# Cross attention on one core: the transposed probabilities' parts are made ahead of the second piece of the token-major context

## The chip, the core and the metric

The kernel runs on one core of a Trainium2 chip. The metric is the device time of one execution in microseconds, as the median of several runs.

## The reference, cut to what matters

The whole network is a layer norm, a decoder layer (self attention, cross attention over a context, feed-forward) and a two-expert gated feed-forward, for 8 batches of 100 tokens of width 512. The change touches the cross attention:

```
cscores = einsum('btd,bmd->btm', q1, k2) / sqrt(512)         # 8 x 100 x 722
ca      = einsum('btm,bmd->btd', softmax(cscores), v2)       # memory: 8 x 722 x 512
x       = _ln(x + ca, g2, be2)
```

The kernel multiplies the context itself with the probabilities first, and applies the value weights later (its unit U_CV).

## The kernel before

Nearly every fp32 operand is split in two parts, a high one (rounded to the matmul's format, made by ScalarE with a copy) and a low one (the operand minus the high part, made by DVE or POOL with a subtraction), and each product is three matmuls: high x high, high x low, low x high. Names end in H and L for the parts and in R for what was loaded.

The cross attention is a loop over the 8 batches b. Each engine has its program written out by hand, in order, and the engines wait for each other by semaphores only. For a batch the context is used twice: feature-major (ctR, ctH, ctL; two pieces) for the scores, and token-major (cnR, cnH, cnL; three pieces of 256 token rows, i = 0, 1, 2) for the value product. There is one buffer each of cnR, cnH and cnL, and two of ctH and ctL.

- TensorE (block `tensor`): `cross_attend(b)`, the value product, 18 matmuls at L750 to L752, six for each piece of cn; then `cross_prob_transpose(b + 1)` (L737, 6 transposes), `cross_scores(b + 2)` (L724 to L726, 24 matmuls; from b = 6 on half of the unit U_CV instead, 24 matmuls at L576 to L578), and `cross_attend_transpose(b)` (L762, 4 transposes).
- ScalarE: `split_cn` copies cnR to cnH (L919), `cross_attended` scales the value product into utok (L1011), `cross_probT` copies the transposed probabilities to ptH (L1003), `split_ct` makes ctH (L912), `cross_exp` the exponential prob (L995), `cross_attendedT` AH (L1016).
- DVE: `split_cn` makes cnL of pieces 0 and 1 (L1179), `cross_recip` srec (L1341), `cross_probT` the low part ptL of the transposed probabilities (L1335), `cross_max` the maximum in three small instructions, the last of which writes snb (L1327, L1328, L1330), `split_ct` ctL (L1174), `cross_attendedT` AL (L1345).
- POOL makes cnL of piece 2 (L493), one per batch from batch 1 on.
- SP issues the loads: a piece of cnR or ctR is asked for when its low part has been made from the piece before.

The value product of batch b waits for ptL of batch b at its start, and for each piece's cnL as it comes to it:

```python
def cross_attend(b):
    pe.wait_ge(c_probT_low, b + 1)
    ...
    for c in range(MC):
        wait_cn_low(pe, b, c // 2)
```

`wait_cn_low` waits for POOL's count for piece 2 and for DVE's count for pieces 0 and 1. ScalarE's copy into cnH waits for the piece's transfer and for the chunks of the value product before that read the same piece. utok waits for all six chunks of its batch. The exponential of a batch waits for snb.

Of the kernel before, what the change touches and what calls it, by code (L numbers as in the profile page):

```python
# [113 lines left out]
def build(nc, x, ctxt, ctxn, wvo, wts, consts, g3, be3, out):  # L114
    with ExitStack() as ctx:
# [203 lines left out]
        def raw(ap):  # L319
            return ap.bitcast(F32)  # L320
# [565 lines left out]
        def _(act):  # L886
            def split_weights(n, k):
                raw_weights = WRK if n == U_K else WR
                if n == U_Q and k == 0:
                    act.wait_ge(w0_loaded, 16)  # L890
                elif n == U_Q and k == 2:
                    act.wait_ge(weights_loaded, 16)
                elif n == U_K:
                    act.wait_ge(wk_loaded, 16)
                elif k == 0:
                    act.wait_ge(weights_loaded, 16 * LOADED.index(n))
                if k == 0 and BEFORE[n] is not None:
                    m, h = ORDER[LAST[BEFORE[n]]]
                    act.wait_ge(gemm_done, gemm_count(m, h, KC - 1))
                elif k == 0 and SLOT[n] == 2:  # L900
                    act.wait_ge(ct_low, 2 * B)
                    for i in (1, 2):
                        wait_cn_low(act, B - 1, i)
                act.activation(WH[SLOT[n]][:, k, :], raw_weights[:, k, :], ACT.Copy).then_inc(w_high, 1)  # L904

            def split_ct(b, i):
                act.wait_ge(ct_loaded[i], 16 * (b + 1))
                if b == 1:
                    act.wait_ge(to_feat, 16)
                if b >= 2:  # L910
                    act.wait_ge(c_scores, b - 1)
                act.activation(ctH[b % 2][:, 2 * i:2 * i + 2, 0:M], ctR[:, 2 * i:2 * i + 2, :],  # L912
                               ACT.Copy).then_inc(ct_high, 1)

            def split_cn(b, i):
                act.wait_ge(cn_loaded[i], (16 if i < 2 else 48) * (b + 1))
                if b >= 1:
                    act.wait_ge(c_chunk, MC * (b - 1) + 2 * i + 2)
                act.activation(cnH[:, 2 * i:2 * i + 2, :], cnR[:, 2 * i:2 * i + 2, :],  # L919
                               ACT.Copy).then_inc(cn_high, 1)  # L920

            def unit(n, h, groups=range(KC)):
                for e in groups:
                    src = ps[:, bank(n, h, e), 0:HALF]
                    kind = KINDS[n]
                    if act_writes(n):
                        act.wait_ge(gemm_done, gemm_count(n, h, e))
                    if kind == "fp32":
                        dst, col = (qT, C_BQ) if n == U_Q else (kT, C_BK)
                        act.activation(half(dst, h, e), src, ACT.Identity,  # L930
                                       bias=cst[:, col + e:col + e + 1]).then_inc(act_evac, 1)
                    elif kind == "split":
                        act.activation(half(AH, h, e), src, ACT.Identity, bias=gv[:, e:e + 1]).then_inc(act_evac, 1)
                    elif kind == "relu_bias":
                        col = C_B1 + KC * ((n - U_F) // 2) + e
                        act.activation(half(AT, h, e), src, ACT.Relu, bias=cst[:, col:col + 1])  # L936
                        act.activation(half(AH, h, e), src, ACT.Relu,  # L937
                                       bias=cst[:, col:col + 1]).then_inc(act_evac, 1)
                    elif kind == "relu":
                        act.activation(half(AH, h, e), src, ACT.Relu).then_inc(act_evac, 1)  # L940
                    if POS[n, h] in SPLIT_AT:
                        for k in [[0, 1], [2], [3], []][e]:
                            split_weights(SPLIT_AT[POS[n, h]], k)
# [47 lines left out]
            def cross_exp(b):  # L991
                act.wait_ge(c_max, b + 1)
                if b >= 2:
                    act.wait_ge(c_probT, b - 1)
                act.activation(prob[b % 2][:, 0:M].rearrange("p (i m) -> p i m", i=2), ps[0:T, 4:6, 0:MH],  # L995
                               ACT.Exp, bias=snb[:, b:b + 1], scale=SCALE,
                               accum_out=ssum[:, b:b + 1]).then_inc(c_exp, 1)

            def cross_probT(b):
                act.wait_ge(c_probT, b + 1)  # L1000
                if b >= 2:
                    act.wait_ge(c_chunk, MC * (b - 1))
                act.activation(ptH[b % 2][:, :].rearrange("p (i m) -> p i m", i=2), ps[:, 6:8, 0:3 * T],  # L1003
                               ACT.Copy).then_inc(c_probT_high, 1)

            def cross_attended(b):
                act.wait_ge(c_chunk, MC * (b + 1))
                act.wait_ge(c_rec, b + 1)
                if b >= 2:
                    act.wait_ge(c_attT, b - 1)  # L1010
                act.activation(utok[:, b % 2, :], ps[0:T, 2, :], ACT.Copy,  # L1011
                               scale=srec[:, b:b + 1]).then_inc(c_att_sb, 1)

            def cross_attendedT(b):
                act.wait_ge(c_attT, b + 1)
                act.activation(tokens(AH, b), ps[:, 3, 0:KC * T].rearrange("p (k t) -> p k t", k=KC),  # L1016
                               ACT.Copy).then_inc(c_attT_high, 1)
# [66 lines left out]
            for b in range(B):  # L1084
                if b + 1 < B:
                    split_cn(b + 1, 0)
                    split_cn(b + 1, 1)
                cross_attended(b)
                if b + 1 < B:
                    cross_probT(b + 1)  # L1090
                    split_cn(b + 1, 2)
                if b + 3 < B:
                    split_ct(b + 3, 0)
                if b + 2 >= B:
                    unit(U_CV, 0, [[0, 1], [2, 3]][b + 2 - B])
                if b + 2 < B:
                    cross_exp(b + 2)
                if b + 3 < B:
                    split_ct(b + 3, 1)
                cross_attendedT(b)  # L1100
                if b == B - 2:
                    for k in range(KC):
                        split_weights(U_F, k)
# [53 lines left out]
        def _(dve):  # L1157
# [14 lines left out]
            def split_ct(b, i):  # L1172
                dve.wait_ge(ct_high, 2 * b + i + 1)
                dve.tensor_tensor(ctL[b % 2][:, 2 * i:2 * i + 2, 0:M], ctR[:, 2 * i:2 * i + 2, :],  # L1174
                                  raw(ctH[b % 2][:, 2 * i:2 * i + 2, 0:M]), ALU.subtract).then_inc(ct_low, 1)

            def split_cn(b, i):
                dve.wait_ge(cn_high, 3 * b + i + 1)
                dve.tensor_tensor(cnL[:, 2 * i:2 * i + 2, :], cnR[:, 2 * i:2 * i + 2, :],  # L1179
                                  raw(cnH[:, 2 * i:2 * i + 2, :]), ALU.subtract).then_inc(cn_low, 1)  # L1180
# [152 lines left out]
            def cross_probT(b):  # L1333
                dve.wait_ge(c_probT_high, b + 1)
                dve.tensor_tensor(ptL[b % 2][:, :].rearrange("p (i m) -> p i m", i=2), ps[:, 6:8, 0:3 * T],  # L1335
                                  raw(ptH[b % 2][:, :].rearrange("p (i m) -> p i m", i=2)),
                                  ALU.subtract).then_inc(c_probT_low, 1)

            def cross_recip(b):
                dve.wait_ge(c_exp, b + 1)  # L1340
                dve.reciprocal(srec[:, b:b + 1], ssum[:, b:b + 1]).then_inc(c_rec, 1)  # L1341
# [179 lines left out]
            for b in range(B):  # L1521
                if b + 1 < B:
                    split_cn(b + 1, 0)
                    split_cn(b + 1, 1)
                    cross_recip(b + 1)
                    cross_probT(b + 1)
                if b + 2 < B:
                    cross_max(b + 2)
                if b + 3 < B:
                    split_ct(b + 3, 0)  # L1530
                if b + 2 >= B:
                    unit(U_CV, 0, [[0, 1], [2, 3]][b + 2 - B])
                if b + 3 < B:
                    split_ct(b + 3, 1)
                cross_attendedT(b)
# [87 lines left out]
```

## Time and profile before

| | us |
|---|---|
| median of 3 runs | 532.81 (532.42 to 533.29) |
| profiled execution, its own time | 532.86 |
| span of its trace (first to last instruction) | 531.1 |
| TensorE matmul busy | 519.0 (98% of the span) |
| VectorE (DVE) busy | 325.7 (61%) |
| ScalarE (ACT) busy | 222.0 (42%) |
| GpSimd (POOL) busy | 104.1 (20%) |

The loop of the cross attention lies between about 140 and 214 us of the span. The granted TensorE clock is full (1.00) there. Times in the rows below are microseconds from the start of the span. A row of the timeline gives the start, the duration, the engine, the line, the operation, output<-inputs, and in brackets how long the engine had been idle before it and what released it; where several instructions alike follow each other they are one row with their count. A busy TensorE in these rows is not TensorE at its peak: its matmuls overlap in the records, and starts are what to go by.

### The profile page before, as it was taken

What the parts mean: (1) busy time and instruction counts of PE and PEld (TensorE: products, weight loads), DVE (VectorE), ACT (ScalarE), POOL (GpSimd) and SP (SyncE); (2) the same over time, 40 slices, a digit from 0 to 9 for tenths busy, and PEclk for the clock granted to TensorE, in tenths of its full rate; (3) what the DMA queues carried; (4) which work ended last, traced back from release to release, by engine and by line L of the source; (5) the groups of instructions that cost most, each with busy time, mean ns of one, the idle gap of its engine ahead of it and who ended that gap; (6) DMA issues with size and microseconds to landing.
All of it is one profiled execution on the core that took longest, in us unless ns stands there. A gap on an engine that the chain in (4) does not pass through costs nothing.

```text
span 531.1 us, 7541 instructions
## 1 busy us (share of the span) xinstructions
PE 519.0 (98%) x3014; PEld 496.3 (93%) x3014; DVE 325.7 (61%) x556; ACT 222.0 (42%) x388; POOL 104.1 (20%) x93
## 2 busy tenths in 40 slices
PE   8899999999999999999999999999999999999996
PEld 6799999789988878999999999999999899999996
DVE  3753789895698986877365544277674354442225
ACT  2853542483589865264535153206413231320200
POOL 2430430022032135054006200005530000000000
PEclk9999999999999999999999999999999999999999
DMA  8941212031589961228022222002220033100004
GB/s 231 349 166 57 64 73 79 1 113 56 192 287 325 305 224 34 79 97 227 1 79 80 80 80 79 1 0 81 80 79 1 0 123 117 53 28 0 1 1 123
DMA packets 18428, 53.75 MB, mean 101 GB/s; under 512 B 1625, under 2 KB 2425, under 8 KB 15833
## 3 DMA queue, kind: packets, MB, share of 16 engines
q1 hardware_dynamic: 18332, 53.20, 30.6%
q8 instruction: 24, 0.39, 0.3%
q10 hardware_dynamic: 60, 0.07, 0.1%
q14 instruction: 12, 0.09, 0.1%
HBM read 51.63 MB, written 1.64 MB: 100 GB/s over the span
## 4 chain that ended last, share of the span: by engine, by line
PE 81%; DVE 11%; DMA 3%; ACT 3%; issue 2%; SPq 0%; POOL 0%; DVEq 0%; ACTq 0%
PE ps L576 21%; PE ps L578 21%; PE ps L577 21%; PE ps L611 3%; DMA tok<-x_in 2%; PE ps L589 2%; DVE cnL L1179 2%; PE ps L750 1%; DMA cnR<-ctxn_in 1%; PE ps L752 1%; PE ps L751 1%; PE ps L622 1%; PE ps L724 1%; PE ps L726 1%; PE ps L725 1%
## 5 line engine op out<-in xcount | busy, mean ns | idle before, releaser
L576 PE MATMUL ps<-XH,WH 128*128 128x400 f32 x352 | 122.5, 348 | 0.9 <-DVE AL L1191 0.4
L578 PE MATMUL ps<-XH,WL 128*128 128x400 f32 x352 | 121.5, 345 | 0.0
L577 PE MATMUL ps<-XL,WH 128*128 128x400 f32 x352 | 121.4, 345 | 0.0
L576 PE MATMUL ps<-AH,WH 128*128 128x400 f32 x288 | 100.2, 348 | 0.6 <-DVE AL L1195 0.2
L578 PE MATMUL ps<-AH,WL 128*128 128x400 f32 x288 | 99.4, 345 | 0.0
L577 PE MATMUL ps<-AL,WH 128*128 128x400 f32 x288 | 99.3, 345 | 0.0
L576 PEld LDWEIGHTS ps<-XH,WH 128*128 128x128 f32 x352 | 66.1, 188 | 2.7 <-DVE AL L1191 0.8
L577 PEld LDWEIGHTS ps<-XL,WH 128*128 128x128 f32 x352 | 66.2, 188 | 0.1
L578 PEld LDWEIGHTS ps<-XH,WL 128*128 128x128 f32 x352 | 66.2, 188 | 0.0
L488 POOL TENSOR_TENSOR WL<-WR,WH 128x512 fp32r<-128x512 f32 x38 | 52.4, 1409 | 67.2 <-ACT WH L904 67.2
L576 PEld LDWEIGHTS ps<-AH,WH 128*128 128x128 f32 x288 | 54.1, 188 | 2.1 <-DVE AL L1195 1.9
L577 PEld LDWEIGHTS ps<-AL,WH 128*128 128x128 f32 x288 | 54.1, 188 | 0.0
L578 PEld LDWEIGHTS ps<-AH,WL 128*128 128x128 f32 x288 | 54.1, 188 | 0.0
L1213 DVE TENSOR_TENSOR acc<-ps,acc 128x400 f32<-128x400 f32 x48 | 27.3, 571 | 40.4 <-PE ps L578 40.1
L904 ACT ACTIVATE WH<-WR 128x512 fp32r<-128x512 f32 x80 | 45.9, 627 | 13.5 <-DMA WR<-wts_in 13.5
L936 ACT ACTIVATE AT<-ps,cst 128x400 f32<-128x400 f32 x32 | 19.1, 596 | 76.3 <-PE ps L578 76.2
L940 ACT ACTIVATE AH<-ps 128x400 fp32r<-128x400 f32 x32 | 16.1, 504 | 81.0 <-PE ps L578 81.0
L1198 DVE SCALAR_TENSOR_TENSOR AL<-ps,AH 128x400 fp32r<-128x400 f32 x32 | 18.4, 575 | 42.3 <-ACT AH L940 42.3
L1195 DVE TENSOR_TENSOR AL<-AT,AH 128x400 fp32r<-128x400 f32 x32 | 21.4, 670 | 36.3 <-ACT AH L937 36.1
L1174 DVE TENSOR_TENSOR ctL<-ctR,ctH 128x1444 fp32r<-128x1444 f32 x16 | 26.6, 1660 | 14.2 <-ACT ctH L912 14.2
L1169 DVE TENSOR_TENSOR WL<-WR,WH 128x512 fp32r<-128x512 f32 x40 | 29.9, 767 | 6.4 <-ACT WH L904 6.4
L493 POOL TENSOR_TENSOR cnL<-cnR,cnH 128x1024 fp32r<-128x1024 f32 x7 | 16.8, 2401 | 65.9 <-ACT cnH L919 65.9
(181 smaller groups left out, 817.8 us busy)
## 6 DMA issues: line engine op xcount, KB each, us to landing
WR<-wts_in SPq DMA_DIRECT2D x19, 1024.0 KB, 4.8
ctR<-ctxt_in SPq DMA_DIRECT2D x16, 722.0 KB, 5.0
cnR<-ctxn_in SPq DMA_DIRECT2D x16, 512.0 KB, 5.2
cnR<-ctxn_in SPq DMA_DIRECT2D x8, 256.0 KB
tok<-x_in SPq DMA_DIRECT2D x4, 384.0 KB, 10.4
tok<-x_in SPq DMA_DIRECT2D x1, 1536.0 KB
cnR<-ctxn_in SPq DMA_DIRECT2D x8, 160.0 KB
VR<-wvo_in SPq DMA_DIRECT2D x4, 256.0 KB, 6.2
```

What stands on the lines that cost most here:

```text
L488: pool.tensor_tensor(WL[SLOT[n]][:, k, :], WR[:, k, :], raw(WH[SLOT[n]][:, k, :]), ALU.subtract).then_inc(w_low_pool, 1)
L493: pool.tensor_tensor(cnL[:, 2 * i:2 * i + 2, :], cnR[:, 2 * i:2 * i + 2, :], raw(cnH[:, 2 * i:2 * i + 2, :]), ALU.subtract).then_inc(cn_lo ...
L576: pe.matmul(dst, wh, half(mh, h, k), start=(k == 0), stop=False)
L577: pe.matmul(dst, wh, half(ml, h, k), start=False, stop=False)
L578: mm = pe.matmul(dst, wl, half(mh, h, k), start=False, stop=(k == KC - 1))
L904: act.activation(WH[SLOT[n]][:, k, :], raw_weights[:, k, :], ACT.Copy).then_inc(w_high, 1)
L936: act.activation(half(AT, h, e), src, ACT.Relu, bias=cst[:, col:col + 1])
L1169: dve.tensor_tensor(WL[SLOT[n]][:, k, :], raw_weights[:, k, :], raw(WH[SLOT[n]][:, k, :]), ALU.subtract).then_inc(w_low, 1)
L1174: dve.tensor_tensor(ctL[b % 2][:, 2 * i:2 * i + 2, 0:M], ctR[:, 2 * i:2 * i + 2, :], raw(ctH[b % 2][:, 2 * i:2 * i + 2, 0:M]), ALU.subtrac ...
L1195: dve.tensor_tensor(half(AL, h, e), half(AT, h, e), raw(half(AH, h, e)), ALU.subtract).then_inc(dve_evac, 1)
L1198: dve.scalar_tensor_tensor(out=half(AL, h, e), in0=src, scalar=0.0, in1=raw(half(AH, h, e)), op0=ALU.max, op1=ALU.subtract).then_inc(dve_e ...
L1213: dve.tensor_tensor(half(acc, h, e), src, half(acc, h, e), ALU.add).then_inc(dve_evac, 1)
```

## The change

It moves one piece of work on two engines. On ScalarE the copy of piece 1 (cnH) of the next batch goes from before utok to behind ptH. On DVE the subtraction of piece 1 (cnL) goes from before srec and ptL to behind them. TensorE's, POOL's and SP's programs are untouched, and so is all arithmetic.

```diff
@@ scalar, the loop
             for b in range(B):
                 if b + 1 < B:
                     split_cn(b + 1, 0)
-                    split_cn(b + 1, 1)
                 cross_attended(b)
                 if b + 1 < B:
                     cross_probT(b + 1)
+                    split_cn(b + 1, 1)
                     split_cn(b + 1, 2)
@@ vector, the loop
             for b in range(B):
                 if b + 1 < B:
                     split_cn(b + 1, 0)
-                    split_cn(b + 1, 1)
                     cross_recip(b + 1)
                     cross_probT(b + 1)
+                    split_cn(b + 1, 1)
                 if b + 2 < B:
                     cross_max(b + 2)
```

On DVE, here one iteration of the loop (b = 1; ctL and ptL carry the number of their buffer, "x2" is two instructions alike):

```order
 L1174 TENSOR_TENSOR ctL_79<-ctR,ctH_77 128x2x722 x2
 L1345 TENSOR_TENSOR AL_65<-ps,AH_63 128x4x100
-L1179 TENSOR_TENSOR cnL<-cnR,cnH 128x1024 x2
+L1179 TENSOR_TENSOR cnL<-cnR,cnH 128x1024
 L1341 RECIPROCAL srec<-ssum 100x1
 L1335 TENSOR_TENSOR ptL_86<-ps,ptH_84 128x600
+L1179 TENSOR_TENSOR cnL<-cnR,cnH 128x1024
 L1327 TENSOR_REDUCE smx<-ps 100x1
 L1328 TENSOR_SCALAR smx<-smx,cshift 100x1
```

The second cnL now stands between ptL and the maximum. On ScalarE, the same iteration before the change, from one exponential (prob) to the next:

```order
L995 ACTIVATE prob_82,ssum<-ps,snb 100x722
L912 ACTIVATE ctH_77<-ctR 128x2x722
L1016 ACTIVATE AH_63<-ps 128x4x100
L919 ACTIVATE cnH<-cnR 128x1024 x2
L1011 ACTIVATE utok<-ps,srec 100x512
L1003 ACTIVATE ptH_84<-ps 128x600
L919 ACTIVATE cnH<-cnR 128x1024
L912 ACTIVATE ctH_76<-ctR 128x2x722
L995 ACTIVATE prob_83,ssum<-ps,snb 100x722
```

and with the change:

```order
L995 ACTIVATE prob_82,ssum<-ps,snb 100x722
L912 ACTIVATE ctH_77<-ctR 128x2x722
L1016 ACTIVATE AH_63<-ps 128x4x100
L919 ACTIVATE cnH<-cnR 128x1024
L1011 ACTIVATE utok<-ps,srec 100x512
L1003 ACTIVATE ptH_84<-ps 128x600
L919 ACTIVATE cnH<-cnR 128x1024 x2
L912 ACTIVATE ctH_76<-ctR 128x2x722
L995 ACTIVATE prob_83,ssum<-ps,snb 100x722
```

utok and ptH move forward by one cnH, and the second cnH stands directly ahead of the third.

## Rows read from the trace of the kernel before

**Rows 1.** Windows, each one iteration, from one value product's start to the next's.

```profile
core 0: us, PE busy (x) PEld busy (x) DVE busy (x) ACT busy (x) POOL busy (x), PEclk, DMA share, GB/s
149.40:158.38 8.98, 8.98 (x55) 7.72 (x54) 8.16 (x11) 6.89 (x10) 2.16 (x2) 1.00 0.98 320
...
176.92:186.97 10.05, 9.22 (x52) 7.77 (x52) 9.23 (x11) 8.82 (x12) 3.21 (x2) 1.00 0.90 305
...
196.11:205.52 9.41, 9.41 (x54) 8.17 (x53) 7.52 (x10) 5.33 (x8) 3.95 (x2) 1.00 0.43 148
```

**Rows 2.** Line L750: what ended its engine's idle time (us, times).

```profile
  DVE ptL L1335: 2.2, 3
```

**Rows 3.** Timeline of TensorE: starts of value products and of thirteenth matmuls.

```profile
167.57 0.47 PE L750 MATMUL ps<-cnH,ptH 128*100 128x512 f32 x1
...
170.42 0.39 PE L750 MATMUL ps<-cnH,ptH 128*100 128x512 f32 x1
...
186.97 0.47 PE L750 MATMUL ps<-cnH,ptH 128*100 128x512 f32 x1 [0.84 <-DVE ptL L1335]
...
198.95 0.39 PE L750 MATMUL ps<-cnH,ptH 128*100 128x512 f32 x1
```

**Rows 4.** Timeline of ScalarE: exponentials, and the work between two of them.

```profile
150.85 0.87 ACT L995 ACTIVATE prob<-ps,snb 100x722 f32<-100x722 f32 x1 [1.25 <-DVE snb L1330]
...
160.07 0.87 ACT L995 ACTIVATE prob<-ps,snb 100x722 f32<-100x722 f32 x1
...
160.92 1.40 ACT L912 ACTIVATE ctH<-ctR 128x1444 fp32r<-128x1444 f32 x1
...
162.60 2.00 ACT L919 ACTIVATE cnH<-cnR 128x1024 fp32r<-128x1024 f32 x2
164.50 0.68 ACT L1011 ACTIVATE utok<-ps,srec 100x512 f32<-100x512 f32 x1
...
169.23 0.87 ACT L995 ACTIVATE prob<-ps,snb 100x722 f32<-100x722 f32 x1 [0.22 <-DVE snb L1330]
...
173.79 1.06 ACT L919 ACTIVATE cnH<-cnR 128x1024 fp32r<-128x1024 f32 x1 [0.96 <-DMA cnR<-ctxn_in]
...
198.35 0.86 ACT L995 ACTIVATE prob<-ps,snb 100x722 f32<-100x722 f32 x1 [2.52 <-DVE snb L1330]
```

**Rows 5.** Timeline of POOL in the same iteration: piece 2 of cnL.

```profile
166.77 2.41 POOL L493 TENSOR_TENSOR cnL<-cnR,cnH 128x1024 fp32r<-128x1024 f32 x1 [6.75 <-ACT cnH L919]
```

**Rows 6.** Timeline of DVE in the same iteration.

```profile
164.42 2.35 DVE L1179 TENSOR_TENSOR cnL<-cnR,cnH 128x1024 fp32r<-128x1024 f32 x2
...
166.76 0.76 DVE L1335 TENSOR_TENSOR ptL<-ps,ptH 128x600 fp32r<-128x600 f32 x1
167.44 0.90 DVE L1327 TENSOR_REDUCE smx<-ps 100x1 f32<-100x722 f32 x1
...
168.62 0.58 DVE L1330 SCALAR_TENSOR_TENSOR snb<-cshift,smx 100x1 f32<-100x1 f32 x1
```

**Rows 7.** The chain of work that ended last: transfer of a second piece.

```profile
166.79 6.97 DMA cnR<-ctxn_in
```

**Rows 8.** Timeline elsewhere, and L535 (min/median/max ns): POOL beside DVE with two SBUF inputs.

```profile
283.74 0.69 DVE L1169 TENSOR_TENSOR WL<-WR,WH 128x512 fp32r<-128x512 f32 x1
283.81 1.77 POOL L535 TENSOR_TENSOR tok<-tok,be3b 100x512 f32<-100x512 f32 x1 [37.40 <-PE ps L578]
...
L535 POOL TENSOR_TENSOR tok<-tok,be3b x8: 1274/1684/1768, 283.8 to 294.3; 100x512 f32<-100x512 f32 x8
...
228.28 1.30 POOL L488 TENSOR_TENSOR WL<-WR,WH 128x512 fp32r<-128x512 f32 x1 [7.86 <-ACT WH L904]
228.94 1.07 DVE L1207 TENSOR_TENSOR XS<-XS,XL 128x400 f32<-128x400 f32 x1
229.54 1.62 POOL L488 TENSOR_TENSOR WL<-WR,WH 128x512 fp32r<-128x512 f32 x1
```

## The prediction

> **What bounds the kernel now.** I read the windows of the cross attention loop first. TensorE is busy in practically all of each iteration, so a microsecond is only won where TensorE waits. An iteration in which it waits for nothing takes 8.98 us (149.40 to 158.38, four products of scores, value product, transposes) [rows 1]. The four iterations from 158.38 to 196.11 take 37.73 us, where 4 x 8.98 is 35.92: 1.8 us are lost in them, the most in the one of 10.05 us [rows 1]. The idle time before the value product's matmuls (L750) is put down to one releaser, the low part ptL of the transposed probabilities, 2.2 us over both of TensorE's queues in three places [rows 2], one of them 0.84 us [rows 3]. That is what the change goes for. The next question is what makes ptL late.
>
> Write E(k) for the start of the exponential of batch k on ScalarE. The starts run from 150.85 (k=2) to 198.35 (k=7), with 160.07 and 169.23 between [rows 4]: 47.50 us for five steps, 9.50 each, more than TensorE's 8.98. So another loop is the slower one. One step of it, from 160.07 to 169.23, is 9.16 us, and ScalarE, POOL and DVE pass it on: the exponential, ctH at +0.85, AH, the first two pieces of cnH from +2.53 (162.60), utok and ptH from +4.43 (164.50), the third piece of cnH [rows 4], then POOL's cnL of that piece from 166.77 (+6.70) for 2.41 us, to 169.18 [rows 5], and the exponential of the next batch at 169.23. What ties the last two is DVE's snb: a 100x1 instruction issued at 168.62 that takes 0.58 us and ends at 169.20, right after POOL [rows 6]. It reads two tensors in SBUF while POOL reads SBUF, and does not get through before POOL is done. So E(k+1) = POOL's end + 0.05. ptL ends 7.45 us after E(k) (166.76 + 0.76 against 160.07) [rows 6], and TensorE begins the value product of batch k at 167.57, which is E(k) + 7.50 [rows 3]. Of the 1.70 us by which five steps exceed 5 x 9.16, the rest are steps in which ScalarE waits for the second piece's transfer: it took 6.97 us [rows 7] and kept the copy 0.96 us [rows 4]. At k=2 and k=7 TensorE is behind this loop, between them it goes at the loop's pace.
>
> **The change part by part.** Nothing is added: the same instructions in another order, for b+1 = 1 to 7. On ScalarE the copy of the second piece goes behind utok and ptH. Those three together take as long as before, the third piece's copy ends where it did, and POOL is released at E + 6.70 as before. utok moves forward to about E + 3.5 and waits there for the value product of the batch before, which began at 158.38 [rows 1] and takes 4.2 us (2.85 us for twelve of its eighteen matmuls [rows 3]): done near 162.7, and wanted at 163.5. No new wait. On DVE the second cnL goes behind srec and ptL. The four instructions (cnL, cnL, srec, ptL) run from 164.42 to the start of the maximum at 167.44 in either order. So in the new order ptL is done one cnL earlier, about 1.13 us (half of the pair's 2.27 step), at E + 6.32; and cnL of the second piece ends where ptL ended, about E + 7.46, after beginning at about E + 6.24 [rows 6]. TensorE needs that piece six matmuls into the product, 1.42 us after its start, E + 7.79 at the earliest: 0.3 us to spare. SP's queue asks for the next second piece 0.75 us later than before, but ScalarE wants it 1.14 us later, so the 0.96 us wait of [rows 4] goes. A rest of it up to 0.6 us would cost nothing, because DVE takes the piece at E + 6.24 only.
>
> **The price.** Before, DVE was in ptL (one input in PSUM) when POOL began, and neither minded the other. Now DVE is in a cnL, two inputs in SBUF, from E + 6.24 to E + 7.46 when POOL is released at E + 6.70. No row of before has this pair, but two have its kind. At 283.74 DVE begins a WL of two SBUF inputs and keeps its usual 0.69 us; POOL's sum, released at 283.81, takes 1.77 us where the shortest of its eight is 1.274. DVE's end at 284.43 lies 0.62 into it: 0.50 us longer for an overlap of 0.62 [rows 8]. At 229.54 POOL takes 1.62 instead of 1.30, with DVE's end at 230.01, 0.47 into it: 0.32 us longer [rows 8]. So POOL is held by the overlap less 0.12 to 0.15. Here the overlap is 0.76 us, and the hold 0.62 us. (The Trainium skill, "SBUF — State Buffer", section "Who interferes with whom", says that a DVE instruction with two SBUF inputs contends with a GpSimd instruction that reads SBUF, that whoever issues first has the pair for the whole instruction, and that the other blocks. The rows agree in kind; by the page the hold would be the whole overlap, which is a rival below.)
>
> Through snb the hold enters the slower loop: each step becomes 9.16 + 0.62 = 9.78 us. It is paid six times (the pieces of batches 1 to 6), and the two waits for transfers go. E(7) = 150.85 + 6 x 0.62 + 5 x 9.16 = 200.37, against 198.35. ptL being early doesn't help there: TensorE begins the product of batch k at E(k) + 6.37 at best, and its third piece (the thirteenth matmul, 2.85 us in, as 167.57 to 170.42 shows [rows 3]) is wanted at E(k) + 9.22, while POOL delivers it at E(k) + 9.73. Before, it was wanted at E(k) + 10.35 and there at 9.11. So the wait moves from ptL to POOL's piece, some 0.5 us in each of batches 3 to 6. From the thirteenth matmul of batch 6 (198.95) to the start of batch 7's product (205.52) TensorE works 6.57 us [rows 1, 3]. Now that stretch starts at E(7), as POOL is done then: 200.37 + 6.57 = 206.94, **1.42 us later** than 205.52. Behind that TensorE is continuously busy and sets the pace, so it stays. The profiled execution took 532.86 us (its span is 531.1), and the median of the runs is 532.81, so both can stand as the base: 532.86 + 1.4 = 534.3 us.
>
> **Bounds of the unknown.** The sum moves by six times the hold. With the whole overlap of 0.76 it is +2.3 us, 535.1. With 0.5 it is +0.7. The break-even is 0.62 - 1.42/6 = 0.38 us. With no hold TensorE binds: 158.38 + 4 x 8.98 + 9.41 = 203.70, or -1.8 us. I take 0.62 because two rows of different lengths give the same rule and the pair here differs only in being longer.
>
> **The rivals.**
> (1) *POOL isn't held by this pair, and the gain comes through*: ptL 1.13 us early removes TensorE's waits, 1.8 us, 531.1 us. For it: TensorE's idle time is really put down to ptL [rows 2], and the change does bring ptL forward. Against it: both rows of the kind show POOL longer. It decides where the hold is under 0.38 us. Chance 0.18.
> (2) *A smaller hold, 0.2 to 0.5 us*, because the second cnL begins earlier against POOL than worked out (the hold shrinks as ScalarE is later): the gain at ptL and the loss at POOL cancel, 532.3 to 533.5. Chance 0.20.
> (3) *The full overlap counts*, by the page's rule worked out on these rows as 0.76 us: 535.1 us. Chance 0.12. The same page gives about 115 ns between the end of the DVE instruction and the release; as an estimate by that page the sum would be some 0.7 us more again.
> (4) *The order turns round*: if POOL were released before DVE begins the second cnL (0.46 us of margin), DVE would stand for POOL's 2.41 us, and the maximum with it. One such step costs some 2.4 us: 536.5. snb shows that DVE does stand [rows 6]. Chance 0.03.
> The forecast, a hold of 0.5 to 0.75 us, has the other 0.47.
>
> **How the numbers follow.** About 0.2% (1.07 us) is what a measurement of this kernel tells from no change; the three runs spread over 0.9 us. Faster is rival 1 and a tail of 2: 0.20. Same is the rest of 2 and that part of the forecast with a hold under 0.56 us: 0.33. Slower is the rest of the forecast with rivals 3 and 4: 0.47. The predicted time is 534.3, the likeliest case's own range 533.5 to 535.1. The range that leaves out rival 1's end and rival 4 is 531.7 to 535.6.
>
> **What the profile would show.** Right: POOL's cnL (L493) some 3.0 us instead of 2.4 in batches 1 to 6, DVE's second cnL unchanged; the starts of the exponential 9.7 to 9.8 us apart, the last near 200.4; no wait for the second piece's transfer; TensorE idle ahead of the thirteenth value matmul and no longer ahead of the first. Wrong: POOL's cnL still at 2.4 us and the exponentials at 9.2 us (rival 1), or DVE's second cnL at over 3 us (rival 4). It would also be wrong if transfers, asked for later, came later than ScalarE wants them; then ScalarE's waits for DMA would grow, and they would show by name.

## The result, and the profile after

| | before | after |
|---|---|---|
| median of 10 runs each, us | 532.62 | 533.69 |
| ratio, 95% interval | | 1.0023 (1.0013 to 1.0032) |
| span of the profiled execution, us | 531.1 | 532.4 |

The change costs about 1.2 us by the ratio (0.7 to 1.7 us by its interval); the two medians are 1.07 us apart. The loop says more than the total. First POOL's part in it, the seven instructions that make piece 2 of cnL, in the timeline of the changed kernel:

```profile
147.51 2.93 POOL L493 TENSOR_TENSOR cnL<-cnR,cnH 128x1024 fp32r<-128x1024 f32 x1 [24.93 <-ACT cnH L919]
157.20 3.02 POOL L493 TENSOR_TENSOR cnL<-cnR,cnH 128x1024 fp32r<-128x1024 f32 x1 [6.76 <-ACT cnH L919]
166.98 3.00 POOL L493 TENSOR_TENSOR cnL<-cnR,cnH 128x1024 fp32r<-128x1024 f32 x1 [6.76 <-ACT cnH L919]
...
196.49 3.01 POOL L493 TENSOR_TENSOR cnL<-cnR,cnH 128x1024 fp32r<-128x1024 f32 x1 [6.75 <-ACT cnH L919]
204.96 2.50 POOL L493 TENSOR_TENSOR cnL<-cnR,cnH 128x1024 fp32r<-128x1024 f32 x1 [5.46 <-ACT cnH L919]
```

Six of the seven take 2.93 to 3.02 us where [rows 5] has 2.41. What holds them stands on DVE, here in the step of the third of them:

```profile
165.83 0.76 DVE L1335 TENSOR_TENSOR ptL<-ps,ptH 128x600 fp32r<-128x600 f32 x1
166.51 1.21 DVE L1179 TENSOR_TENSOR cnL<-cnR,cnH 128x1024 fp32r<-128x1024 f32 x1
...
168.82 1.18 DVE L1330 SCALAR_TENSOR_TENSOR snb<-cshift,smx 100x1 f32<-100x1 f32 x1
```

The second cnL begins at 166.51, POOL is released at 166.98 and ends at 169.98, 0.6 us later than it would alone; snb, issued at 168.82, ends at 170.00. ptL is done at 166.59, 6.32 us after its exponential, where before it was done after 7.45, one cnL later. The exponentials on ScalarE, with the longest of the waits for transfers between them:

```profile
150.50 0.87 ACT L995 ACTIVATE prob<-ps,snb 100x722 f32<-100x722 f32 x1 [1.77 <-DVE snb L1330]
...
160.27 0.87 ACT L995 ACTIVATE prob<-ps,snb 100x722 f32<-100x722 f32 x1 [1.13 <-DVE snb L1330]
...
168.97 1.41 ACT L912 ACTIVATE ctH<-ctR 128x1444 fp32r<-128x1444 f32 x1 [2.07 <-DMA ctR<-ctxt_in]
170.29 0.84 ACT L995 ACTIVATE prob<-ps,snb 100x722 f32<-100x722 f32 x1
...
180.03 0.87 ACT L995 ACTIVATE prob<-ps,snb 100x722 f32<-100x722 f32 x1 [0.86 <-DVE snb L1330]
...
189.80 0.86 ACT L995 ACTIVATE prob<-ps,snb 100x722 f32<-100x722 f32 x1 [1.85 <-DVE snb L1330]
...
199.56 0.87 ACT L995 ACTIVATE prob<-ps,snb 100x722 f32<-100x722 f32 x1 [3.14 <-DVE snb L1330]
```

The steps are 9.77, 10.02, 9.74, 9.77 and 9.76 us. The waits for the second piece of cnR (0.96 us in [rows 4], and one of 0.49) are gone. Those for ctR are three now, 0.60, 2.07 and 0.86 us, where before they were two, 1.00 and 0.91; the one of 2.07 makes the step of 10.02. In sum ScalarE waits as long for transfers as before, 3.5 us against 3.4. And what TensorE waits for at the value product, as line L750 has it (us, times):

```profile
  POOL cnL L493: 5.0, 9
```

It was ptL, 2.2 us, in [rows 2]. (Both counts go over TensorE's two queues, so one wait can stand in them twice.) The waits stand at the thirteenth matmul, as in this row of its timeline:

```profile
170.03 0.48 PE L750 MATMUL ps<-cnH,ptH 128*100 128x512 f32 x1 [0.39 <-POOL cnL L493]
```

Windows of both traces from the start of batch 1's value product to that of batch 7's give the loop's sum: 57.69 us now, 56.12 before (149.40 to 205.52), 1.57 us more. The rest of the difference of the two spans isn't the loop's: this execution came to the loop 0.87 us earlier (148.53 against 149.40), and it spent 0.6 us more in the last stretch, 32.40 us at a granted clock of 0.97, where before the same stretch (499.30 to 531.10) took 31.80 us at 1.00:

```profile
148.53:206.22 57.69, 56.15 (x315) 46.24 (x314) 51.47 (x60) 44.07 (x58) 18.22 (x7) 1.00 0.79 259
...
500.00:532.40 32.40, 28.14 (x166) 27.39 (x164) 12.85 (x24) 2.02 (x4) 0.00 (x0) 0.97 0.17 51
```

### The profile page after: what moved, and what is told of

Read it like the earlier page. It is cut to its first block, busy times and chain, and to the rows that moved or that the text cites. A ratio compares the mean times of both kernels' runs of the same rounds, so it can differ in the third digit from the quotient of the medians.

```text
span 532.4 us, 7541 instructions
## 1 busy us (share of the span) xinstructions
PE 519.7 (98%) x3014; PEld 495.1 (93%) x3014; DVE 328.1 (62%) x556; ACT 221.5 (42%) x388; POOL 106.9 (20%) x93
## 4 chain that ended last, share of the span: by engine, by line
PE 75%; DVE 9%; ACT 5%; DMA 3%; issue 3%; POOL 3%; SPq 1%; DVEq 0%; ACTq 0%
PE ps L576 20%; PE ps L578 20%; PE ps L577 20%; PE ps L611 3%; POOL cnL L493 2%; DMA WR<-wts_in 2%; ACT cnH L919 2%; DMA OR<-wvo_in 2%; PE ps L589 2%; PE ps L750 1%; PE ps L752 1%; PE ps L751 1%; PE ps L622 1%; PE ps L724 1%; PE ps L726 1%
## 5 line engine op out<-in xcount | busy, mean ns | idle before, releaser
L493 POOL TENSOR_TENSOR cnL<-cnR,cnH 128x1024 fp32r<-128x1024 f32 x7 | 20.5, 2925 | 64.4 <-ACT cnH L919 64.4
```

The lines of the kernel that those rows point to most:

```text
L493: pool.tensor_tensor(cnL[:, 2 * i:2 * i + 2, :], cnR[:, 2 * i:2 * i + 2, :], raw(cnH[:, 2 * i:2 * i + 2, :]), ALU.subtract).then_inc(cn_lo ...
```

## The experiments

Theory A: the hold on POOL, carried by snb to the next exponential. Theory B: the loss comes from the transfers, which are asked for later. All ratios are to the kernel before on the same chip. "Five steps" is the time from the exponential of batch 2 to that of batch 7 in the profiled execution: 47.50 us before, 49.06 after.

| kernel | ratio (95%) | five steps, us | POOL's cnL, median us |
|---|---|---|---|
| e1 DVE's part alone | 1.0061 (1.0043 to 1.0079) | 49.68 | 3.19 |
| e2 ScalarE's part alone | 1.0005 (0.9993 to 1.0017) | 47.08 | 2.49 |
| e3 before, snb in another form | 0.9988 (0.9978 to 0.9999) | 45.77 | 2.40 |
| e4 after, snb in another form | 1.0012 (0.9998 to 1.0026) | 49.37 | 3.01 |
| e5 half of the second cnL behind ptL | 1.0133 (1.0104 to 1.0161) | 54.65 | 2.39 |
| e6 after, second cnL in two | 1.0044 (1.0029 to 1.0060) | 49.15 | 3.07 |
| e7 before, half the context's bytes | 0.9986 (0.9973 to 1.0000) | 45.80 | 2.40 |
| e8 after, half the bytes | 1.0026 (1.0014 to 1.0038) | 48.81 | 3.00 |
| e9 e7 and snb's form | 0.9966 (0.9954 to 0.9979) | 44.89 | 2.41 |
| e10 e8 and snb's form | 0.9968 (0.9955 to 0.9981) | 44.88 | 3.01 |
| e11 e2 and snb's form | 0.9989 (0.9977 to 1.0001) | 45.37 | 2.50 |

### The two halves of the change (e1, e2)

e1 takes the vector hunk of the diff alone, e2 the scalar hunk alone.

> The change on DVE alone; ScalarE's order is that of before. Theory A (the hold: DVE's second cnL holds POOL's cnL by 0.6 us, and snb, which waits for POOL's end, carries that to the next exponential) expects POOL's cnL at 3.0 us in six batches and exponentials at least 9.78 us apart, so at least the 1.1 us that the whole change lost; and more where the second piece's transfer lands late, since ScalarE now wants it before utok again while it is asked for 0.75 us later: 533.5 to 536. Theory B (the loss is that of the transfers asked for later, the hold costs nothing) expects the same later transfers to show as waits of the copy of the second piece and POOL's hold to leave no mark: 533 to 535 with exponentials 9.2 us apart wherever no transfer is waited for.

> The change on ScalarE alone; DVE's order is that of before (both cnL ahead of srec and ptL). DVE wants the second cnH at 5.5 us after the exponential and gets it at 5.6, so ptL is as late as before, the second cnL is done when POOL starts, and there is no hold. Theory A expects POOL's cnL at 2.4 us, steps of 9.2 us, the waits for the second piece's transfer gone (worth up to 1.7 us at the exponentials), and a time 0 to 1.2 us below before. Theory B expects about the same, as the request for the second piece moves by 0.1 us only.

e1 loses more than the whole change, though no copy of the second piece waits for its transfer. In its timeline, DVE's second cnL and POOL's:

```profile
157.26 1.22 DVE L1179 TENSOR_TENSOR cnL<-cnR,cnH 128x1024 fp32r<-128x1024 f32 x1
```

```profile
157.56 3.19 POOL L493 TENSOR_TENSOR cnL<-cnR,cnH 128x1024 fp32r<-128x1024 f32 x1 [6.75 <-ACT cnH L919]
```

In ScalarE's old order ptH comes one cnH later, so DVE's second cnL begins 0.16 us later after the exponential (6.40 against 6.24). The overlap is 0.92 us instead of 0.74, the hold 0.78 instead of 0.60, and the steps are 9.93 to 9.95 us. The size of the hold sets the step, as theory A has it; the expected waits for the second piece did not come. Four waits for ctR did (0.51 to 1.42 us), but each of these steps still ends with ScalarE waiting for snb. e2 has next to no hold (2.49 us: cnL ends 0.2 us after POOL's release), its steps are 9.25 us until transfers of ctR interfere (9.78, 9.57), and no gain can be told from zero. So the loss is in DVE's half, and with ScalarE's half it is smaller.

### Cutting the carrier (e3, e4)

```diff
-                dve.scalar_tensor_tensor(out=snb[:, b:b + 1], in0=cshift[:, b:b + 1], scalar=SCALE,
-                                         in1=smx[:, b:b + 1], op0=ALU.mult, op1=ALU.add).then_inc(c_max, 1)
+                dve.tensor_scalar(snb[:, b:b + 1], cshift[:, b:b + 1], SCALE, smx[:, b:b + 1], ALU.mult,
+                                  ALU.add).then_inc(c_max, 1)
```

> The kernel of before with one instruction in another form: snb made by a tensor_scalar with cshift as the only SBUF tensor input and smx as its per-partition scalar, so that it need not wait for POOL (the instruction ahead of it, of that form, took its usual 0.21 us beside POOL). Same arithmetic. Theory A expects snb at 0.2 us, the exponentials free of POOL's end, the step set by TensorE (9.0 us) or by the transfers, and 0.8 to 1.8 us less than before. If snb is held in this form as well, the time is that of before.

> The changed kernel with snb in the form of the run before. Theory A expects POOL's cnL still held, at about 3.0 us, but no loss from it: exponentials free of POOL, ptL early, 0.8 to 1.8 us less than before, thus 2 to 3 us less than the changed kernel. Theory B (later transfers) expects that this form brings no more than it brings to the kernel before, so that the changed kernel stays 1 us behind it.

Line L1330, in the changed kernel and in e3 (min/median/max ns):

```profile
L1330 DVE SCALAR_TENSOR_TENSOR snb<-cshift,smx x8: 159/1167/1180, 132.2 to 198.4; 100x1 f32<-100x1 f32 x8
```

```profile
L1330 DVE TENSOR_SCALAR snb<-cshift,smx x8: 214/214/217, 133.1 to 196.3; 100x1 f32<-100x1 f32 x8
```

The new form never stands for POOL. e3 gains 0.6 us, less than expected; in its trace ScalarE waits 4.9 us for transfers in all, 3.4 before. e4 does not do what theory A said: it is 0.0011 below the changed kernel, as e3 is 0.0012 below before, which is what theory B had expected (0.0011 is less than the two intervals allow to tell from nothing). Its profiled execution, the slowest of its twelve, shows a place where a gain can be lost. ScalarE waits at ctH:

```profile
169.88 1.41 ACT L912 ACTIVATE ctH<-ctR 128x1444 fp32r<-128x1444 f32 x1 [3.32 <-DMA ctR<-ctxt_in]
...
188.69 1.41 ACT L912 ACTIVATE ctH<-ctR 128x1444 fp32r<-128x1444 f32 x1 [2.09 <-DMA ctR<-ctxt_in]
```

The transfer engines' share is 0.96 between 150 and 190 us already before, so there is little room for a faster loop. These two runs alone could not tell A from B. They do show something of their own: e4 stays 0.0024 of the time, 1.2 us, behind e3 (medians 532.47 and 531.29 on one chip; drawing anew from the runs gives 0.5 to 1.8 us). So with snb cut loose and full loads the change still costs time, and by another way than snb.

### Taking the transfers away (e7 to e10)

```diff
+                    mw = M if b < 3 else MH
-                    sp.dma_start(ctR[:, 2 * i:2 * i + 2, :],
-                                 ctxt[b, 2 * P * i:2 * P * (i + 1), :].rearrange("(k p) m -> p k m", p=P)
+                    sp.dma_start(ctR[:, 2 * i:2 * i + 2, 0:mw],
+                                 ctxt[b, 2 * P * i:2 * P * (i + 1), 0:mw].rearrange("(k p) m -> p k m", p=P)
...
+                    dw = D if b < 2 else D // 2
-                    sp.dma_start(cnR[:, 2 * i:2 * i + full, :],
-                                 ctxn[b, 2 * P * i:2 * P * i + full * P, :].rearrange("(c p) d -> p c d", p=P)
+                    sp.dma_start(cnR[:, 2 * i:2 * i + full, 0:dw],
+                                 ctxn[b, 2 * P * i:2 * P * i + full * P, 0:dw].rearrange("(c p) d -> p c d", p=P)
```

> The kernel of before with half the context's bytes moved: from batch 3 on only the first 361 of 722 columns of the feature-major context are loaded, from batch 2 on only the first 256 of 512 of the token-major one; the rest of each buffer keeps the values of an earlier batch. All other work is the same. No copy waits for a transfer any more. Theory A (hold through snb) expects steps of 9.16 us throughout and 1.0 to 1.3 us less than before. Theory B (transfers alone) expects the same or a little more of a gain.

> The changed kernel with the same halved loads. Theory A expects no help from them: steps of 9.77 us, POOL at 3.0 us, TensorE at the thirteenth matmul, 1.2 to 1.6 us more than before and 2.3 to 2.8 us more than the light kernel before. Theory B (the loss is transfers asked for later) expects it to fall to the light kernel before, within 0.3 us.

> The light kernel before with snb in the form with one SBUF tensor input. Neither POOL nor the transfers set the step, so TensorE does: steps of 9.0 us, 1.5 to 2.0 us less than before. That it gained only 0.6 us with full loads would then be the transfers' doing.

> The light changed kernel with snb in that form. Theory A expects POOL's cnL still at 3.0 us and all the same the time of the run before, 1.4 to 2.0 us less than before, thus 2.6 to 3.6 us less than the light changed kernel: the hold costs time through snb alone. If POOL's lateness costs in another way too (ctL's subtraction, which also reads two SBUF tensors, held longer behind it), it stays 0.5 us or more behind the run before.

Two lines were added ahead of these places, so L495, L752, L997 and L1332 below are L493, L750, L995 and L1330 of the other kernels. With light transfers the kernel before steps at 9.15 to 9.17 us (45.80 for five), and the changed one at 9.76, with nothing on ScalarE waiting for DMA. Between 140 and 206 us the changed one's ScalarE waits only for snb, but for some of TensorE's work at the two ends of the loop:

```profile
ACT prob L997 <- DVE snb L1332: 15.6, 7, 3.4
```

and on TensorE's two queues:

```profile
PEld ps L752 <- POOL cnL L495: 3.5, 5, 0.9
PE ps L752 <- POOL cnL L495: 1.5, 4, 0.4
```

The difference of the two is 0.0040 of the time, 2.1 us, and 3.0 us in the five steps, where with full loads it was 0.0023 and 1.56 us: the change costs no less when transfers are no issue. (That it costs more is what the two pairs of traces say; the intervals of the runs leave it open.) Theory B falls as the cause of the loss. With snb in the new form on top, both come to 44.9 us (8.98 a step, TensorE's own pace [rows 1]) and to the same time, though POOL is held as much as ever (line L495 of e10, min/median/max ns):

```profile
L495 POOL TENSOR_TENSOR cnL<-cnR,cnH x7: 2490/3006/3017, 148.0 to 201.4; 128x1024 fp32r<-128x1024 f32 x7
```

The hold costs nothing once snb doesn't carry it. (DVE's next instruction that reads two SBUF tensors, ctL, now stands for POOL: its longest takes 2.385 us in e10 against 1.775 in e9, and the time is the same.) e9 and e10 against e7 and e8 show theory A. They also say what kept e4 behind e3: with halved loads that difference is gone, so it hangs on the transfers. Theory B's cost is there, behind the hold, and shows when the hold no longer costs. By which wait the change brings it about was not tried.

### Who comes first (e5, e6)

```diff
+            def split_cn_half(b, c):
+                dve.wait_ge(cn_high, 3 * b + 2)
+                half_cn = dve.tensor_tensor(cnL[:, c, :], cnR[:, c, :], raw(cnH[:, c, :]), ALU.subtract)
+                if c == 3:
+                    half_cn.then_inc(cn_low, 1)
...
                     split_cn(b + 1, 0)
-                    split_cn(b + 1, 1)
+                    split_cn_half(b + 1, 2)
                     cross_recip(b + 1)
                     cross_probT(b + 1)
+                    split_cn_half(b + 1, 3)
```

That is e5, against the kernel before. e6 has both halves behind `cross_probT`, and ScalarE's part of the change.

> DVE's second cnL in two instructions of 128x512; the first of them ahead of srec and ptL, the second behind, ScalarE's order that of before. The second half would begin 6.85 us after the exponential, 0.15 us after POOL is released, so POOL is first. Theory A with whole instructions (rival 4 of the prediction) expects POOL at 2.4 us, the half cnL standing some 2.3 us (2.9 us instead of 0.65), exponentials 11.0 us apart, and about 9 us more than before, 540 to 543. If the two engines shared the port, or POOL were held by half a cnL whoever begins, it would be 0 to 1.5 us more than before.

> The changed kernel with DVE's second cnL in two instructions of 128x512 back to back behind ptL. POOL is released 0.15 us before the first of them ends. If the waiting POOL gets the port at that boundary, POOL's cnL takes 2.4 to 2.5 us, the second half of the cnL stands for it, and the time is some 9 us above before, as with one half moved. If DVE keeps the port over the boundary, POOL takes 3.0 to 3.1 us and the time is that of the changed kernel, 533.7 to 534.3.

Two steps of e5, first DVE's moved half, then POOL:

```profile
147.45 0.68 DVE L1184 TENSOR_TENSOR cnL<-cnR,cnH 128x512 fp32r<-128x512 f32 x1
...
157.28 2.79 DVE L1184 TENSOR_TENSOR cnL<-cnR,cnH 128x512 fp32r<-128x512 f32 x1
```

```profile
147.40 2.99 POOL L493 TENSOR_TENSOR cnL<-cnR,cnH 128x1024 fp32r<-128x1024 f32 x1 [24.90 <-ACT cnH L919]
157.14 2.38 POOL L493 TENSOR_TENSOR cnL<-cnR,cnH 128x1024 fp32r<-128x1024 f32 x1 [6.75 <-ACT cnH L919]
```

At 157.28 POOL was 0.14 us ahead, and half a cnL took 2.79 us instead of 0.68; the steps are 10.93 us and the kernel 7 us slower. At 147.45 POOL was only 0.05 us ahead in the records, and it was the one that was held. The 9 us expected were too many, in the main because this first round was not of the expensive kind; the step, 11.0 expected, came out 0.07 lower. In e6 the two halves ran as one (1.28 us) and POOL, waiting at their boundary, took 3.07: it did not get in between them. (The Trainium skill, "SBUF — State Buffer", section "Who interferes with whom", says that issue order and not the shape of the operation decides who blocks. e5 agrees where the starts are 0.14 us apart: the same half cnL that ran in 0.68 us stood 2.1 us. Where they are 0.05 us apart, the order of the recorded starts does not tell who was first.)

### A version that might beat both (e11)

The scalar hunk of the change and snb's new form on the kernel before.

> A version that may beat both: ScalarE's order of the change (which takes the waits for the second piece's transfer away), DVE's order of before (no hold), snb with one SBUF tensor input (no coupling to POOL), full loads. With both waits gone TensorE or the transfers set the step; 0.6 to 1.6 us less than before. If the transfers bind as with snb alone, no better than 0.6 us.

Five steps take 45.37 us, less than e3's, and TensorE is busy throughout 150 to 190 us; but the ratio, 0.9989, is about e3's, and its interval reaches past 1. ScalarE still waits 1.7 us for ctR. Of the kernels with full loads only e3 is below before by more than its interval, by 0.1%.

## Why the prediction was right, point by point

- **What bounds the loop.** The circle exponential, ScalarE, POOL, snb at 9.16 us is confirmed by e7, which steps at just that once the transfers don't wait, and by e9, in which the circle is cut and the step falls to TensorE's 8.98.
- **The hold.** Put at 0.62 from two other pairs, it is 0.60 in the loop (3.00 to 3.02 us against 2.41), and 0.52 in the first round, which the sum had at 0.62 too. The working from the rows (overlap less 0.12 to 0.15) was right and not lucky: e1, with 0.92 us of overlap, is held by 0.78.
- **The step.** 9.78 was said, 9.74 to 9.77 measured in four of five. The fifth, 10.02, has a wait for a transfer of ctR that no step of the prediction had: asked for at 161.84, it was there at 168.97, 7.1 us later, where before one asked for at 161.67 was there at 167.60, after 5.9 us. Why it took longer was not tried and stays open.
- **The waits that go.** Those for the second piece went. The waits for ctR, which the prediction did not name though before had two of them, grew from 1.9 to 3.5 us; only 0.25 us of them reached a step.
- **Where the wait goes on TensorE.** From ptL at the first matmul to POOL's piece at the thirteenth, in four batches, as said: in batch 3 the thirteenth begins 3.38 us after the first (166.65 to 170.03), 0.53 us more than the 2.85 without a wait, where some 0.5 was forecast.
- **The sum.** The loop grew by 1.57 us; the sum had 1.42. That they are so close is in part luck, as the 0.25 us for ctR, which the sum did not have, and the 0.10 us too much for the first round go against each other. In the runs the change costs 0.0023 of the time, 1.2 us; 533.69 us lies 0.6 under the 534.3 that was said, of which 0.24 is the base (532.86 was taken, the runs had 532.62). That DVE's half alone costs 3.2 us (e1) is more than the sum gives for its hold of 0.78 (6 x 0.78 in place of 6 x 0.62, 2.4 us); its interval begins at 2.3 us.
- **The rivals.** That POOL isn't held fell with the trace. The full overlap fell too: 0.74 of overlap holds 0.60, so neither the whole overlap nor a further 0.1 us behind DVE's end is paid (the 115 ns that the prediction took from the Trainium skill's page "SBUF — State Buffer" stand there for DMA descriptors that GpSimd writes, not for a subtraction). The turned order, priced at 2.4 us for a step, did not come up here; e5 brought it about at 1.8 us a step (10.93 against 9.16), with half a cnL left to do behind POOL's end; the 2.4 us were for a whole one, 0.5 us more.

The transfers were the weak place of the working: it has them as a stall that goes or stays. e3, e4 and e11 wait for them in their traces, and the 1.2 us between e3 and e4, which halved loads take away, show them as the next bound right behind the hold.

## What to carry to other kernels

A low-priority instruction moved behind an urgent one may now overlap another engine's work, and then it is that engine's chain that pays: look at what runs at the new place, not only at what gets done earlier. Before a reorder, follow the loop that really sets the pace through every engine; here it went through a 100x1 instruction whose duration (0.58 us instead of 0.2) gave the coupling away. When a fix brings less than its mechanism says, take the next resource away (here half the bytes) before dropping the mechanism.

## What the runs showed of the hardware that was not expected

Where a POOL and a DVE instruction start within 0.05 us of each other, the order of the recorded starts does not tell which of them is held. In the first round of e5 DVE, recorded 0.05 us after POOL, ran its usual 0.68 us and POOL was held (2.99 us). In the changed kernel, later in the trace, POOL's sum and a DVE instruction with two SBUF inputs start 0.02 us apart, in the same order (the POOL row is three instructions alike):

```profile
284.49 4.57 POOL L535 TENSOR_TENSOR tok<-tok,be3b 100x512 f32<-100x512 f32 x3 [37.37 <-PE ps L578]
```

```profile
284.51 1.82 DVE L1169 TENSOR_TENSOR WL<-WR,WH 128x512 fp32r<-128x512 f32 x1
```

Here DVE stood: 1.82 us instead of 0.69. e7 has the same pair 0.05 us apart, and DVE stood too (1.79 us). From 0.14 us on DVE stood in all five such steps of e5. What decides below that was not tried.

Two DVE instructions back to back keep POOL waiting over their boundary (3.07 us against 3.00 for one of the same size).
